# Turning x with VectorE's 32x32 block transposes and quarter-row loads, in a graph layer with residual and layer norm

## The reference

```
x: 100000 x 64 f32;  src, dst: 50000 edges, sorted by dst;  edge_attr: 50000 x 32
msg = concat([x[src], edge_attr]) @ W1 + b1            # 50000 x 128
agg = segment_sum(msg, dst, 100000)                    # 100000 x 128
y   = x + concat([x, agg]) @ W2 + b2
out = (y - mean(y)) / sqrt(var(y) + 1e-5)              # over the 64 columns
```

## Time and profile before

| | us |
|---|---|
| median of 3 runs | 1029.17 |
| lowest, highest | 1028.0, 1034.58 |
| the profiled execution | 1031.75 |
| its span, first to last instruction | 1030.0 |
| granted TensorE clock, mean over the span | 0.73 of full |

### The profile page before, as it was taken

How to read it: one execution, slowest core, us unless ns; L and a number is a source line. 1 busy time by engine, 2 the same in 40 slices (tenths; PEclk the granted TensorE clock), 3 DMA queues, 4 the chain that set the end, 5 groups by cost and what they waited for, 6 DMA issues and landing times.

```text
span 1030.0 us, 25989 instructions
## 1 busy us (share of the span) xinstructions
PE 667.1 (65%) x8086; PEld 601.0 (58%) x8087; DVE 411.6 (40%) x945; ACT 446.2 (43%) x2113; POOL 398.7 (39%) x422
## 2 busy tenths in 40 slices
PE   3194557657656775676575677657656756579764
PEld 3174556547646664565475567546646646579753
DVE  7273334334325333333343234533433433337443
ACT  1013434535536454354364346534534534366422
POOL 8664443443443335334434433443443443620000
PEclk8576876876768677677687668867877876678666
DMA  2121322322333223223223223332232332233101
GB/s 62 27 53 40 84 61 66 87 71 66 77 80 98 59 74 88 59 69 91 63 76 87 61 66 85 95 74 68 73 82 61 88 76 57 65 80 90 45 22 42
DMA packets 171918, 71.39 MB, mean 69 GB/s; under 512 B 64737, under 2 KB 165615, under 8 KB 171888
## 3 DMA queue, kind: packets, MB, share of 16 engines
q1 hardware_dynamic: 107728, 51.75, 17.3%
q0 software_dynamic: 12544, 12.87, 6.9%
q10 hardware_dynamic: 51616, 6.41, 4.0%
HBM read 45.37 MB, written 25.60 MB: 69 GB/s over the span
## 4 chain that ended last, share of the span: by engine, by line
PE 61%; issue 31%; DVE 2%; another core or an unknown queue 2%; POOL 2%; DVEq 1%; DMA 0%; ACT 0%; ACTq 0%; POOLq 0%
PE ps_y L549 27%; PE ps_y L540 13%; PE ps_z L468 8%; PE ps_x L529 6%; PE ps_t L460 4%; PE ps_y L586 1%; POOL feat L435 1%; PE ps_x L607 1%; PE ps_y L567 1%; DVE onehot_x L962 1%; DMA feat<-in_x,src_idx 0%; DVEq L962 0%; PE ps_y L607 0%; DVEq L240 0%
## 5 line engine op out<-in xcount | busy, mean ns | idle before, releaser
L435 POOL DMA_INDIRECT feat<-in_x,src_idx x392 | 390.1, 995 | 529.3 <-PE ps_t L460 406.3
L549 PE MATMUL ps_y<-z_window,onehot 128*128 128x64 bf16 x5292 | 292.4, 211 | 285.9 <-issue 282.1
L549 PEld LDWEIGHTS ps_y<-z_window,onehot 128*128 128x128 bf16 x5292 | 240.8, 110 | 337.8 <-issue 328.0
L669 ACT ACTIVATE square<-ps_y 128x64 bf16<-128x64 f32 x784 | 162.6, 240 | 401.8 <-PE ps_y L540 399.8
L932 DVE TENSOR_TENSOR onehot<-node_of_col,dst_in_group 128x2304 bf16<-128x2304 bf16 x98 | 133.2, 1359 | 331.1 <-PE ps_y L540 307.2
L540 PE MATMUL ps_y<-wx,x_t 128*128 128x128 f32 x784 | 155.9, 360 | 6.5 <-issue 6.4
L669 ACT ACTIVATION_READ_ACCUMULATOR square<-ps_y 128x1 f32 x784 | 159.6, 225 | 0.0
L540 PEld LDWEIGHTS ps_y<-wx,x_t 128*128 128x128 f32 x784 | 134.8, 259 | 8.2 <-issue 7.6
L468 PE MATMUL ps_z<-wz,feat_t 97*128 97x64 f32 x784 | 100.6, 285 | 4.5 <-issue 4.5
L468 PEld LDWEIGHTS ps_z<-wz,feat_t 97*128 97x128 f32 x784 | 98.7, 204 | 5.6 <-issue 5.2
L812 DVE TENSOR_TENSOR z<-z_rest,z 128x512 f32 (+1 forms) x49 | 33.9, 691 | 134.1 <-ACT z L657 71.8
(11 more groups left out here) (148 smaller groups left out, 244.2 us busy)
## 6 DMA issues: line engine op xcount, KB each, us to landing
xin<-in_x SPq DMA_DIRECT2D x97, 192.0 KB
out<-yout SPq DMA_DIRECT2D x97, 192.0 KB
xin<-in_x SPq DMA_DIRECT2D x99, 64.0 KB
out<-yout SPq DMA_DIRECT2D x99, 64.0 KB
feat<-in_x,src_idx POOLq DMA_INDIRECT x392
feat<-in_edge_attr ACTq DMA_DIRECT2D x97, 64.0 KB
z<-in_src SPq DMA_DIRECT2D x1, 192.0 KB
z<-in_dst SPq DMA_DIRECT2D x1, 192.0 KB
```

The costliest lines, as they stand in the source:

```text
L435: nc.gpsimd.indirect_dma_start(out=feat[h][:, feat_at(k) + c, 0:C], out_offset=None, in_=x[:, :], in_offset=bass.IndirectOffsetOnAxis(ap=s ...
L549: nc.tensor.matmul(ps_y[h][:, col:col + C], onehot[h][:, slot, a, :], z_window[h][:, slot, part * C:(part + 1) * C], start=False, stop=Fal ...
L669: sq = nc.scalar.activation(square[:, q, :], ps_y[h][:, q * C:(q + 1) * C], ACT.Square, accum_out=sumsq[:, h, q:q + 1])
```

## The change

x is no longer loaded as rows of 128 numbers. Quarter i of such a row, 32 numbers or 128 bytes, goes to partition 32 i + r, where r is the row's number within a group of 32 rows m, and to the columns of m. A block transpose of 32x32 tiles by VectorE (L977 of the kernel after) then gives exactly `x_t`. For this a block is loaded with 8 transfers in place of 2, each to 32 partitions: 4 low ones of 128 pieces and 4 high ones of 384 pieces. TensorE's `turn_x` and ScalarE's `keep_x` are gone. VectorE turns the unit's own x, each half behind its one-hots, not a unit ahead; the turn waits for the load and for the last dense matmul of the block before of that half (`y_done`), whose `x_t[h]` it overwrites. `load_x(k, h)` waits for VectorE's turn of unit k-1.

```
+SQ = 32
+        def low_squares(b, i):
+            at = (BLOCKS - 1 - b) * GN
+            rows = x[at:at + GN, :].rearrange("(p a) c -> p (a c)", a=A)
+            return rows[:, i * SQ:(i + 1) * SQ].rearrange("(m r) c -> r m c", r=SQ)
...
             def load_x(k, h):
                 b = 2 * k + h
-                wait_rounds(sp, x_used[h], k)
-                sp.dma_start(xin[h][:, 0, :], low_part(x, b)).then_inc(x_loaded[h], 16)
+                wait_rounds(sp, x_ready[h], k)
+                for i in range(A * C // SQ):
+                    quarter = xin[h][i * SQ:(i + 1) * SQ, :, :]
+                    sp.dma_start(quarter[:, 0, :].rearrange("r (m c) -> r m c", c=SQ), low_squares(b, i)).then_inc(x_loaded[h], 16)
+                    groups = quarter[:, 1:(G if b > 0 else 2), :].rearrange("r g (m c) -> r (g m) c", c=SQ)
+                    sp.dma_start(groups, high_squares(b, i)).then_inc(x_loaded[h], 16)
                 if b == 0:
...
-                else:
-                    sp.dma_start(xin[h][:, 1:G, :], high_part(x, b)).then_inc(x_loaded[h], 16)
...
-            def turn_x(k, h):
-
-                pe.wait_ge(x_loaded[h], 16 * transfers(k + 1, h))
-                wait_rounds(pe, x_ready[h], k)
-                for g in range(G):
-                    tr = nc.tensor.transpose(ps_x[h][:, g * P:(g + 1) * P], xin[h][:, g, :], ident[:, :])
-                tr.then_inc(x_used[h], 1)
...
                 dense(G - 1).then_inc(y_done[h], 1)
-                turn_x(k + 1, h)
...
-            def keep_x(u, h):
-                act.wait_ge(x_used[h], u + 1)
-                nc.scalar.activation(x_t[h][:, :], ps_x[h][:, :], ACT.Copy).then_inc(x_ready[h], 1)
...
+            def turn_x(k, h):
+
+                dve.wait_ge(x_loaded[h], 16 * x_transfers(k + 1, h))
+
+                dve.wait_ge(y_done[h], k + 1)
+                nc.vector.transpose(x_t[h][:, :], xin[h][:, :, :].rearrange("p g c -> p (g c)")).then_inc(x_ready[h], 1)
...
             def unit(u):
                 one_hots(u, 0)
+                turn_x(u, 0)
                 one_hots(u, 1)
+                turn_x(u, 1)
                 normalize(u)
```

More of the change, by code:

```diff
@@ L210, in gnn_residual_layernorm @@
         x_loaded = sem2("x_loaded")
-        x_used = sem2("x_transposed")
-        x_ready = sem2("x_t_ready")
+        x_ready = sem2("x_turned")
         hots_used = sem2("onehots_used")
@@ L267, in high_part, with high_squares, cut_squares, x_transfers @@
             return t[at:at + groups * GN, :].rearrange("(g p a) c -> p g (a c)", g=groups, p=P, a=A)
+        def low_squares(b, i):
+            at = (BLOCKS - 1 - b) * GN
+            rows = x[at:at + GN, :].rearrange("(p a) c -> p (a c)", a=A)
+            return rows[:, i * SQ:(i + 1) * SQ].rearrange("(m r) c -> r m c", r=SQ)
+        def high_squares(b, i):
+            at = LOW + (BLOCKS - 1 - b) * HIGH * GN
+            groups = HIGH if b > 0 else 1
+            rows = x[at:at + groups * GN, :].rearrange("(p a) c -> p (a c)", a=A)
+            return rows[:, i * SQ:(i + 1) * SQ].rearrange("(m r) c -> r m c", r=SQ)
+        def cut_squares(i, m, parts):
+            rows = x[CUT:N, :].rearrange("(p a) c -> p (a c)", a=A)
+            return rows[m * SQ:m * SQ + parts, i * SQ:(i + 1) * SQ]
         def cut_part(t):
             return t[CUT:N, :].rearrange("(p a) c -> p (a c)", a=A)
+        def x_transfers(k, h):
+            return 2 * A * C // SQ * k + (A * C // SQ * -(-CUT_PARTS // SQ) if h == 0 and k > 0 else 0) \
+                if isinstance(k, int) else 2 * A * C // SQ * k + A * C // SQ * -(-CUT_PARTS // SQ) * (1 - h)
         def transfers(k, h):
@@ L318, in load_x @@
                 b = 2 * k + h
-                wait_rounds(sp, x_used[h], k)
-                sp.dma_start(xin[h][:, 0, :], low_part(x, b)).then_inc(x_loaded[h], 16)
-                if b == 0:
-                    sp.dma_start(xin[h][:, 1:2, :], high_part(x, b)).then_inc(x_loaded[h], 16)
-                    sp.dma_start(xin[h][0:CUT_PARTS, 2, :], cut_part(x)).then_inc(x_loaded[h], 16)
-                else:
-                    sp.dma_start(xin[h][:, 1:G, :], high_part(x, b)).then_inc(x_loaded[h], 16)
+                wait_rounds(sp, x_ready[h], k)
[4 more added lines that the diff above has]
+                    sp.dma_start(groups, high_squares(b, i)).then_inc(x_loaded[h], 16)
+                if b == 0:
+                    for i in range(A * C // SQ):
+                        for m in range(-(-CUT_PARTS // SQ)):
+                            parts = min(SQ, CUT_PARTS - m * SQ)
+                            sp.dma_start(xin[h][i * SQ:i * SQ + parts, 2, m * SQ:(m + 1) * SQ],
+                                         cut_squares(i, m, parts)).then_inc(x_loaded[h], 16)
             for h in range(2):
@@ L360, in _ @@
                         load_x(k, h)
-                    else:
-                        sp.wait_ge(x_used[h], PAIRS)
-                        sp.sem_inc(x_loaded[h], 32)
                 if k >= 2:
@@ L611, in _ @@
             pe.wait_ge(s_wready, 3)
-            for h in range(2):
-                turn_x(0, h)
             for h in range(2):
@@ L687, in unit @@
                 keep_y(u, 0)
-                keep_x(u + 1, 0)
                 keep_y(u, 1)
                 root(u)
-                keep_x(u + 1, 1)
             act.sem_inc(s_root)
@@ L719, in _ @@
             edge_round(LAG + 1)
-            for h in range(2):
-                keep_x(0, h)
             act.wait_ge(s_opened, 2)
```

## The result

| | us |
|---|---|
| before, median of 14 runs | 1031.07 |
| after, median of 14 runs | 1025.45 (1021.53 to 1028.01) |
| ratio after / before, 95% interval | 0.994 (0.9921 to 0.9959) |
| forecast | 1001, range 982 to 1026 |
| profiled execution after, its span | 1023.63, 1021.8 |

What follows compares the result with a forecast made beforehand. TensorE was taken to bound nearly the whole span, with gathers setting part of each round. 1031.8 - 40 - 3 - 2 (transposes) + 3 (turns) + 14 (SP) = 1003.8, so 1001 for the median; range 982 to 1026.

Steps and rivals of the forecast that it cites:

- The rounds: TensorE without the L529 transposes, 140 to 940 us: 40 us won, bounds 19 and 53.
- 3 for the groups before 140 us: TensorE's 7 further transpose groups ahead of 140 us: about 3 us won.
- 0 for ScalarE's copies, for the loads and for the turns in ordinary rounds: ScalarE's 100 lost copies, smaller load pieces and VectorE's covered turns: no effect on the time.
- The turn: VectorE's block transpose of 128x512 f32: 0.69 us each, 68 us in all, covered in normal rounds.
- Its 3 us in the tail: Behind 940 us, with VectorE in the chain, about 4 to 5 turns count: 3 us lost.
- rival 2: VectorE's turns stretch GpSimd's gathers: + 18 us, about 1019; chance 0.10.
- the term for SP: L974 waits 3.4 us for free_yout behind SP's loads; uncovered in few units: 10 + 4 us, bounds 0 and 34.
- Rival 1: SP's queue becomes the bound from 1.06 us per issue on: about 1210 us at 1.37; chance 0.09 with rival 5.
- Rival 3: PE's instruction processor and late clock leave 19 of 40 us, SP's waits take 14: 1022; chance 0.12.

Runs made afterwards that it cites:

- h1: Kernel after with free_yout ahead of the loads, on a chip where TensorE crawls beside the gathers: 1002.53 us, 0.9598 of before.
- e1: Kernel after with free_yout ahead of the loads, on a chip without the crawl: 699.61 us, 1.0847 of before.
- e3: Kernel before with each load of x cut into four of 32 columns, 8 transfers a block: 663.58 us, 1.0305 of before.
- padded kernel: Kernel before with 45 matmuls of zeros in the first block of each unit while edge rounds run: 1744.05 us, 1.6953 of before without the pad.

## Why the prediction was wrong

- **The rounds** were right. "43 x 0.6 + 42 x 0.35 = 40 us" up to 940 us and 3 for the groups before 140 us; measured 36.7 up to the last gather round, at 918.5 us of before, of which 1.9 had come by gather round 9 (142.2 and 140.3). 0 for ScalarE's copies, for the loads and for the turns in ordinary rounds also held there: the turn waited 6.1 us in all, and L818 stayed covered, but for 1.19 us in the round of two fast units at 332 us.
- **The turn** at 0.69 us, taken from L974: measured 0.703. Its 3 us in the tail: 1.3 in h1.
- **The gathers** (rival 2, + 18 us): their mean is 997 ns, 995 before, and 0.942 to 0.947 us beside a turn alone. By the Trainium skill (SBUF — State Buffer, "Who interferes with whom") a VectorE instruction with at most one SBUF input, outside the two-port modes, does not contend with GpSimd; the trace agrees. The 0.43 us beside L974 were no measure for the turn: a gather that began inside a pass of the scaling ended some 0.82 us after that pass did, and the seven that began inside a turn would by that measure have taken up to 1.44 us.
- **The step that failed** is the term for SP: "It is not covered in the 3 units behind 940 that still have loads, 3.3 us each, 10 us, and in rounds where two fast units end just before the messages [...]: 4 us together." In its place came 28.5 us, 27 of them by the place of `free_yout` (h1) and 1.3 by the turns. The mechanism was named, and its upper bound of 34 held; its count and its size were wrong. Five steps pay, not three: from unit 43 on, before 940 us too, edge rounds come without TensorE's crawl, since the last round of gathers starts at 881.8 and ends at 891.8. And one step costs 3.7 to 7.6 us in place of 3.3: the whole burst is 3.8 us, two bursts run into each other when the units are short (9.7 us from 918.29 to 928.0), a load of 1.3 to 1.5 us is among them, and TensorE comes back from the wait at the lower clock (0.63 from unit 43 on, 0.72 in the kernel before). Without its 14 us for SP the prediction's sum gives a gain of 42 us, and h1, which takes the wait away, gained 42.5, though on a chip where before is 14 us slower.
- **What the cover is made of** was not asked. The prediction asked where L974 is covered today, and found it covered in a normal round; the cover is TensorE's crawl beside the gathers, and it ends with the last gather. Where it is missing, in the tail and on the chips that don't crawl, the same wait costs 28 us and some 170 us (873.06 against 699.61).
- **Rival 1** (SP's queue as the bound, 1.06 us per issue) was weighed at 0.09 with the round of 18.9 us. Issues stayed at 0.43 to 0.47 us, but for seven of 993. It came true all the same where the round is 11.0 us long: 20 issues of 0.49 are 9.8 us, and with the wait for landed stores SP is the bound of e1.
- **Rival 3** (1022) gave the nearest time by luck: it had the rounds win 19, where they won 36.7, and the waits for SP take 14, where they took 27.

The chances, 0.77 for faster by over 1%, went by a sum in which the tail was a small term; the time fell within 1%, and at the upper edge of the range.

## What to carry to other kernels

A cheap step of a queue, such as freeing a buffer, should not stand behind a burst of issues that it has nothing to do with, least of all when the burst is started by the engine that then waits for the step (about 170 us here, and 18.5 in e3, where another engine starts it). Count what a burst of n issues delays, at 0.48 us each, on every engine that waits for a step behind it, and look first at the stretches where the usual cover (here TensorE's slow stretch) is absent, as a program's tail. A wait that is covered today can come due: the "issue" time of TensorE that covered it was found on some chips only, and on a chip without it the same change made the kernel 36% slower. Here the turn on VectorE pays, 0.9598, with the freeing moved ahead, and only on chips that crawl; on the others nothing tried was below the kernel before.

## What was new about the hardware

The same program takes 1029 to 1045 us on some chips and 644 to 648 on others (before: 1031.07, 1030.87 and 1045.03 against 645.05, 644.25, 647.57 and 646.89). The difference is TensorE: beside GpSimd's gathers it executes one or two short matmuls and then mostly has a gap of 0.5 or 1.2 us without any wait that the profile shows, 282 us in all at L549 in the first trace of before; on the other chips a trace has at most two gaps of over 0.3 us between matmuls of one line. In the padded kernel wide matmuls show gaps of 0.79 and 0.82 us too. The kernels before, after and e1 (as h1) each ran on chips of both kinds, so it isn't the kernel; what makes the chips differ stays open.

A gather was stretched by the scaling L974 only when it began while a pass of it ran: it then ended some 0.82 us after the pass, 1.39 us long for a pass that ended 0.57 us into it. Gathers that began first took 0.94 us with both passes beside them.

Between 5 and 8 of SP's 993 load and store issues took 1.0 to 2.0 us in each trace with the eight-transfer loads of the kernel after, the ones beside them 0.43 to 0.47. The kernels with two transfers a block had 2 or 3 of 394, so it is as rare for a small-piece load as for another. Two of them stood in the bursts from 918 to 928 us, which lie on the path. And the 2048 packets of 128 bytes of a block took little: q1's share rose from 17.3 to 24.9%, with the others 35.7% in all, forecast 36.
